# Block 1's down and gate products made inside the scan, one in each unit

## The chip, the cores and the metric

The kernel runs on one core of one Trainium2 chip. A core has TensorE (matrix products into the banks of PSUM), VectorE, ScalarE (activations), GpSimd (called POOL in the profile, it does not read PSUM) and SyncE, which issues transfers. They run side by side, each in its own order, and wait for one another on semaphores. The metric is the device time of one execution in microseconds. Before the change it is 612.0 us, the median of three runs (608.17 to 615.97).

## The reference, cut to what matters

Two blocks follow one another on `x` of 2 x 512 tokens with 256 channels. Block 0 (attention on sorted keys and a mixture of 64 experts) is not touched. Block 1 takes the normalized `xn` through a recurrence with 32 heads of 8 channels and through a feed-forward part with 640 hidden units, and adds both to `x`:

```python
xk, xv, xr, xg = (x + xx * m for m in (maa_k, maa_v, maa_r, maa_g))   # xx: the token before, less x
r, k, v = xr @ Wr.T, xk @ Wk.T, xv @ Wv.T
g = silu(xg @ Wg.T)
att = rc @ kc * w_mat                          # w_mat: decay below the diagonal, u on it, 0 above
yc = att @ vc + rc @ state * wb
new_state = ws * state + kc * wk @ vc
out = (groupnorm(y) * gamma + beta) * g @ Wo.T
ff = square(relu(xn @ w_fc.T)) @ w_proj.T      # with ternary weights
x = x + out + ff
```

## The kernel before

Tokens lie in eight tiles of 128 (`NT`), four for each of the two sequences. Everything is float32. Each engine's program is written out by hand, and its order is the order of the code; nothing is scheduled.

Ahead of block 1's scan TensorE works through this list. The feed-forward's first product fills hidden units by chunk and sequence (`s_ffp`); ScalarE takes the ReLU of each of the ten pieces into `hf` (`s_relu`) and between them makes the decay tables `wmask` by 32 exponentials. VectorE squares each piece (`square`, `s_sq`). `project_T` then makes keys and receptances with channels on the partitions (`s_kTp`, `s_rTp`), from mixtures that VectorE has made (`mixture(k)`, of x and of the difference `dif`; 0 for keys, 1 for receptances, 2 for values, 3 for gates). VectorE copies the keys out (line 1185) and multiplies the receptances by the decay (1192); ScalarE copies these into `rhead`, four times each with the other heads masked out (803). Then TensorE makes the feed-forward's down product, five matmuls to a tile (line 1311 is the helper `product`, so it stands on many rows), and VectorE adds each from PSUM to `xs` (`x2_add`, 1197). Transposes of the keys (1547), scaled by VectorE (1210), give `kn`; `project(2, ...)` gives the values (copied by ScalarE, 808), `project(3, ...)` the gates, of which ScalarE takes the tanh (813) and VectorE makes the silu (1220). POOL cuts `wmask` above the diagonal in one `affine_select` (591), VectorE puts `u` on its diagonal (1215). Only when all gates are ready does `scores(0)` start.

The scan has 16 units, two to a tile: unit u takes the heads `f = u % 2` of tile `u // 2`. TensorE makes four score products (1575), each on 32 rows of the array with 512 columns into banks 0 to 3; they run at the same time if they may start together. VectorE multiplies each by its mask into a ring (1289, `s_a1`). TensorE then makes the unit's outputs from state and masked scores (1585 and 1591) into bank 4 or 5, and the state product (1603); VectorE updates the state (1226, 1227). TensorE is one unit ahead with scores: unit u + 1's scores stand before unit u's outputs, and each waits for the mask that frees its bank. ScalarE copies the outputs (829); TensorE transposes them once in two units (1611), ScalarE copies these to `xn` (833). The group norm of earlier tiles lies between VectorE's masks: means (1242, 1245), then POOL subtracts (607), ScalarE squares (821), variances (1252, 1255), ScalarE's square root (817), and the scale (1262 to 1272). POOL multiplies by scale, gamma, beta and gate (617 to 623). Unit 8 begins the second sequence: VectorE clears the state (1280) after unit 7's outputs.

Behind the scan the eight gated tiles are transposed, multiplied by `Wo`, added to `xs` (1305) and stored.

Of the kernel before, what the change touches and what calls it, by code (L numbers as in the profile page):

```python
# [21 lines left out]
ALU = mybir.AluOpType  # L22
# [3 lines left out]
P = 128  # L26
# [54 lines left out]
def block_kernel(nc, x, consts, w_qk, w_v, w_gate, w_sh13, w_sh2, w_o0, w_13, w_2, maa, td_row, td_col, u_row,  # L81
# [12 lines left out]
    with ctx:  # L94
# [144 lines left out]
        w_head = carve(2 * DC * D, at=sc_at + 15 * N).rearrange("p (k c n) -> p k c n", k=2, c=DC)  # L239
        rw = v3(carve(2 * N), 2, N)  # L240
# [96 lines left out]
        s_wm1 = sem("decay_tables_exp")  # L337
# [10 lines left out]
        s_ffd = sem("ff_down_in_psum")  # L348
        s_x2 = sem("x2_ready")
# [158 lines left out]
        def _(pool):  # L508
# [77 lines left out]
            for k in range(2):  # L586
# [3 lines left out]
            pool.wait_ge(s_wm1, 1)  # L590
            nc.gpsimd.affine_select(out=wmask, in_=wmask, compare_op=ALU.is_ge, fill=0.0, base=-1,
                                    pattern=[[0, H1], [1, P]], channel_multiplier=-1).then_inc(s_wmc, 1)
# [16 lines left out]
            def gated(t):  # L609
# [14 lines left out]

            for t in range(NT):
# [3 lines left out]
                nc.gpsimd.tensor_copy(dst, vn[:, t, :].rearrange("p (g a c) -> p g a c", g=8, a=4)).then_inc(s_vd, 1)  # L629
                if t >= 2:  # L630
                    centred(t - 2)
                if t >= 3:
                    gated(t - 3)
            centred(NT - 2)
# [6 lines left out]
        def _(act):  # L641
# [137 lines left out]
            for b in range(B):  # L779
# [9 lines left out]
                for f in range(FC):  # L789
# [3 lines left out]
                    for h in range(4 * i, min(4 * i + 4, H1)):  # L793
                        last = nc.scalar.activation(wmask[:, h, :], const("pdist"), ACT.Exp, scale=edrow[:, h:h + 1])  # L794
                        if h == H1 - 1:
                            last.then_inc(s_wm1, 1)
# [46 lines left out]
        def _(dve):  # L843
# [307 lines left out]
            def square(i):  # L1151
                dve.wait_ge(s_relu, i + 1)
                h = hf[:, i % FC, (i // FC) * S:(i // FC + 1) * S]
                nc.vector.tensor_tensor(h, h, h, ALU.mult).then_inc(s_sq, 1)

            for i in range(FC):
                square(i)

# [8 lines left out]
            def mixture(k):  # L1167
                for c in range(DC):
                    ins = nc.vector.scalar_tensor_tensor(mix[:, k % 2, c * N:(c + 1) * N], dif[:, c, :],
# [9 lines left out]
            for i in range(FC, 2 * FC):  # L1179
                square(i)  # L1180

# [518 lines left out]
```

## Time and profile before

| what | us or share |
|---|---|
| median of three runs | 612.0 |
| the profiled execution's time | 605.34 |
| its span, first to last instruction | 603.6 |
| TensorE busy over the span | 75% |
| VectorE | 56% |
| ScalarE | 32% |
| POOL | 57% |
| mean granted TensorE clock | 0.895 of 2.4 GHz |

The profile is one execution. Busy time is the time in which an instruction of an engine was under way; matmuls are pipelined, so a busy TensorE is not one at its peak. A float32 product shows two records to a matmul. The chain of waits is followed back from the last instruction to what released each step. A row of the timeline gives start, length, engine, line and operation, the count, and in brackets the idle time before and what ended it. PEld is TensorE loading weights.

### The profile page before, as it was taken

The numbers are of one execution on the slowest core, as the hardware profiler recorded it, in microseconds if no ns is written. First come the engines' busy times: TensorE is split into PE (matmuls) and PEld (weight loads), VectorE is DVE, ScalarE is ACT, GpSimd is POOL, SyncE is SP. The second block draws the span as 40 slices with busy tenths as digits, with TensorE's granted clock in tenths as the row PEclk, the third lists the DMA queues.
The fourth block names the chain that finished last, engine by engine and source line by source line (L and its number), as shares of the span: only waits on it lengthen the run. The fifth ranks groups of instructions, "written<-read, shape, count | busy, mean of one in ns | idle before, by whom it ended". The sixth has DMA issues, their size and how long they took to land.

```text
span 603.6 us, 8476 instructions
## 1 busy us (share of the span) xinstructions
PE 453.7 (75%) x2288; PEld 281.1 (47%) x2288; DVE 340.7 (56%) x931; ACT 193.6 (32%) x512; POOL 343.3 (57%) x327
## 2 busy tenths in 40 slices
PE   2940860767778878887687778779687998899977
PEld 1620420344445445544455445447533587454545
DVE  4899985134444434444444444433467529598984
ACT  1423220233434334333343334422065413121112
POOL 6057777777777787777777777652123101023544
PEclk9975895599998888888989888989879999799997
DMA  8501618167887878788777777862600000000002
GB/s 307 211 24 32 168 24 222 43 165 170 193 201 187 204 199 190 179 198 208 192 191 204 196 189 190 212 145 62 202 9 2 0 0 1 1 1 2 2 2 70
DMA packets 49152, 75.40 MB, mean 125 GB/s; under 512 B 13721, under 2 KB 30457, under 8 KB 48953
## 3 DMA queue, kind: packets, MB, share of 16 engines
q1 hardware_dynamic: 32136, 53.74, 29.0%
q0 software_dynamic: 16992, 21.38, 19.7%
q8 instruction: 11, 0.18, 0.1%
q14 instruction: 13, 0.10, 0.1%
HBM read 58.31 MB, written 15.99 MB: 123 GB/s over the span
## 4 chain that ended last, share of the span: by engine, by line
POOL 33%; PE 25%; issue 17%; DMA 13%; DVE 8%; ACT 4%; SPq 0%; ACTq 0%; POOLq 0%; DVEq 0%
POOL big L543 15%; PE ps L1311 15%; POOL routed L557 9%; POOL big L550 7%; DMA routed<-big 6%; DMA big<-tok_tab,big 5%; PE ps L1575 4%; DVE big L1289 2%; PE ps L1316 2%; PE ps L1591 2%; DMA big<-in_maa 1%; ACT big L794 1%; DVE big L914 1%; DVE big L911 1%; DVE big L918 1%
## 5 line engine op out<-in xcount | busy, mean ns | idle before, releaser
L1311 PE MATMUL ps<-big 128*128 128x352 f32 (+4 forms) x768 | 223.2, 441 | 2.5 <-ACT big L708 0.9
L1311 PEld LDWEIGHTS ps<-big 128*128 128x128 f32 (+2 forms) x768 | 149.2, 202 | 58.1 <-issue 24.1
L543 POOL DMA_INDIRECT big<-val_tab,big x128 | 123.8, 967 | 62.5 <-issue 38.1
L557 POOL DMA_INDIRECT routed<-big x64 | 103.8, 1621 | 42.5 <-ACT big L718 25.9
L1316 PE MATMUL ps<-cst,big 128*128 128x128 f32 x144 | 31.3, 307 | 80.6 <-DMA big<-tok_tab,big 79.0
L1027 DVE COPY big<-ps 88x256 f32<-88x256 f32 x64 | 26.9, 421 | 91.3 <-PE ps L1403 90.2
L550 POOL DMA_INDIRECT big<-tok_tab,big x64 | 63.1, 986 | 19.5 <-issue 18.6
L1019 DVE SCALAR_TENSOR_TENSOR big<-big,ps 128x176 f32<-128x176 f32 x64 | 21.6, 338 | 84.5 <-ACT big L713 84.5
L708 ACT ACTIVATE big<-ps 128x256 f32<-128x256 f32 x64 | 24.5, 384 | 132.8 <-PE ps L1316 131.9
L1316 PEld LDWEIGHTS ps<-cst,big 128*128 128x128 f32 x144 | 16.7, 148 | 101.1 <-DMA big<-tok_tab,big 78.9
L1311 PE MATMUL ps<-xnT,big 128*128 128x512 f32 (+1 forms) x104 | 50.3, 641 | 2.1 <-ACT xnT L645 2.1
L713 ACT ACTIVATE big<-ps 128x176 f32<-128x176 f32 x64 | 20.3, 317 | 76.5 <-PE ps L1311 76.5
L1289 DVE TENSOR_TENSOR big<-ps,big 128x512 f32<-128x512 f32 x64 | 41.9, 677 | 2.5 <-PE ps L1575 2.1
L1575 PE MATMUL ps<-big 32*128 32x512 f32 x128 | 35.7, 673 | 3.0 <-DVE big L1289 2.0
L724 ACT ACTIVATE big<-ps 128x512 f32<-128x512 f32 x64 | 34.6, 599 | 0.5 <-PE ps L1420 0.4
L1311 PEld LDWEIGHTS ps<-xnT,big 128*128 128x128 f32 (+1 forms) x104 | 20.5, 203 | 27.7 <-issue 26.1
L718 ACT ACTIVATE big<-ps,big 128x256 f32<-128x256 f32 x64 | 30.0, 469 | 8.8 <-PE ps L1311 8.4
L1403 PE MATMUL ps<-cst,big 128*88 128x128 f32 x128 | 28.3, 307 | 0.0
L1316 PE MATMUL ps<-cst,xn 128*128 128x128 f32 x48 | 10.8, 352 | 20.4 <-DVE xn L879 17.7
L1403 PEld LDWEIGHTS ps<-cst,big 128*88 128x88 f32 x128 | 15.6, 134 | 21.1 <-issue 17.2
L596 POOL MEMSET big<- 128x2560 f32 x1 | 2.2, 2236 | 39.2 <-ACT big L808 39.2
L607 POOL TENSOR_TENSOR xn<-xn,gst 128x256 f32<-128x256 f32 x8 | 5.0, 629 | 33.5 <-DVE gst L1245 33.5
(179 smaller groups left out, 616.3 us busy)
## 6 DMA issues: line engine op xcount, KB each, us to landing
big<-in_w SPq DMA_DIRECT2D x64, 352.0 KB
big<-in_w SPq DMA_DIRECT2D x64, 176.0 KB
big<-q_dram SPq DMA_DIRECT2D x144, 32.0 KB
routed<-big POOLq DMA_DIRECT2D x2, 1152.0 KB
big<-val_tab,big POOLq DMA_INDIRECT x128, 2.3
big<-routed SPq DMA_DIRECT2D x4, 512.0 KB, 4.3
q_dram<-big SPq DMA_DIRECT2D x24, 64.0 KB, 1.8
tok_tab<-xn SPq DMA_DIRECT2D x1, 1280.0 KB, 5.2
```

What stands on the lines that cost most here:

```text
L543: nc.gpsimd.indirect_dma_start(vals[:, group, side, c, :], None, val_tab, bass.IndirectOffsetOnAxis(ap=vidxT[:, col:col + 1], axis=0))\
L550: nc.gpsimd.indirect_dma_start(xe[:, e % SLOTS, :], None, tok_tab, bass.IndirectOffsetOnAxis(ap=sidx[:, e:e + 1], axis=0))\
L557: nc.gpsimd.indirect_dma_start(routed[e % 2], bass.IndirectOffsetOnAxis(ap=sidx[:, e:e + 1], axis=0), ye[:, e % 2, :], None, compute_op=AL ...
L708: nc.scalar.activation(xeT[:, u % 2, :, :], PS[0][:, 0:D].rearrange("p (c n) -> p c n", c=DC), ACT.Copy).then_inc(s_xeT, 1)
L718: nc.scalar.activation(ye[:, u % 2, :], PS[3][:, 0:D], ACT.Copy, scale=gate).then_inc(s_y, 1)
L724: nc.scalar.activation(ex[:, c, :], PS[4 + c % 2][:, :], ACT.Exp).then_inc(s_ex, 1)
L1027: nc.vector.tensor_copy(heT[:, u % 2, :, :], PS[2][0:IC, 0:2 * P].rearrange("p (c n) -> p c n", c=2))\
L1289: nc.vector.tensor_tensor(aring[:, a % 8, :].rearrange("p (h n) -> p h n", h=4), PS[q][:, :].rearrange("p (h n) -> p h n", h=4), wmask[:, ...
L1311: last = nc.tensor.matmul(o, w, m, start=(n == 0), stop=(n == len(pairs) - 1))
L1316: last = nc.tensor.transpose(bank[:, c * P:(c + 1) * P], src[:, c * P:(c + 1) * P], ident)
L1403: last = nc.tensor.transpose(PS[2][0:IC, c * P:(c + 1) * P], hm[:, u % 2, c * IC:(c + 1) * IC], ident)
L1575: nc.tensor.matmul(PS[q][:, :], kT[rows, f, tok(t)], rhead[rows, f, :, tok(t)], start=True, stop=True).then_inc(s_a1p, 1)
```

## The change

Two products leave the stretch ahead of the scan. The down product of a tile is made in that tile's first unit and its gate product in the second, between two halves of the next unit's scores: quarters 0 and 1, the product, then quarters 2 and 3. The down product goes to bank 5, the gate product to bank 4, the two output banks, so that outputs now wait for the copy or the gate step that frees them. ScalarE copies the down sums from PSUM to `ffo`, two tiles long, because POOL now adds them to `xs` and can't read PSUM. ScalarE's tanh stands between the copies of the scan, VectorE's gate step behind the first mask of the next even unit. Squares go from VectorE to POOL, and the cut of `wmask` is made in two halves, the diagonals on VectorE likewise. The gates' mixture is written over `xnT`.

```diff
@@ POOL @@
+            def square(i):
+                pool.wait_ge(s_relu, i + 1)
+                h = hf[:, i % FC, (i // FC) * S:(i // FC + 1) * S]
+                nc.gpsimd.tensor_tensor(h, h, h, ALU.mult).then_inc(s_sq, 1)
+            def causal(i):
+                w = wmask[:, i * HH:(i + 1) * HH, :]
+                pool.wait_ge(s_wm1[i], 1)
+                nc.gpsimd.affine_select(out=w, in_=w, compare_op=ALU.is_ge, fill=0.0, base=-1,
+                                        pattern=[[0, HH], [1, P]], channel_multiplier=-1).then_inc(s_wmc, 1)
+            for i in range(4):
+                square(i)
+            causal(0)
+            square(4)
+            causal(1)
+            for i in range(FC, 2 * FC):
+                square(i)
...
-                    pool.wait_ge(s_g, NT)
+                pool.wait_ge(s_g, t + 1)
...
+            def x2_add(t):
+                pool.wait_ge(s_ffo, t + 1)
+                nc.gpsimd.tensor_tensor(xs[:, t, :], ffo[:, t % 2, :], xs[:, t, :], ALU.add).then_inc(s_x2, 1)
...
+                if t >= 1:
+                    x2_add(t - 1)
@@ ACT @@
+            def ff_copy(t):
+                act.wait_ge(s_ffd, t + 1)
+                if t >= 2:
+                    act.wait_ge(s_x2, t - 1)
+                nc.scalar.activation(ffo[:, t % 2, :], PS[5][:, 0:D], ACT.Copy).then_inc(s_ffo, 1)
+            def gate_tanh(t):
                 act.wait_ge(s_gp, t + 1)
-                if t == 0:
-                    act.wait_ge(s_knp, NT)
-                nc.scalar.activation(gn[:, t, :], PS[t % 4][:, 0:D], ACT.Tanh, scale=0.5).then_inc(s_gt, 1)
+                nc.scalar.activation(gn[:, t, :], PS[4][:, 0:D], ACT.Tanh, scale=0.5).then_inc(s_gt, 1)
...
                     u = 2 * t + f
+                    (ff_copy, gate_tanh)[f](t)
                     act.wait_ge(s_yTp, u + 1)
@@ DVE @@
-            for i in range(FC, 2 * FC):
-                square(i)
+            def diagonal(i):
+                dve.wait_ge(s_wmc, i + 1)
+                for h in range(i * HH, (i + 1) * HH):
+                    note(nc.vector.scalar_tensor_tensor(wmask[:, h, :], ident, urow[:, h:h + 1], wmask[:, h, :],
+                                                        ALU.mult, ALU.add))
+            diagonal(0)
...
-            for t in range(NT):
-                x2_add(t)
             mixture(3)
...
+                    if q == 0 and u >= 2 and not f:
+                        gate(u // 2 - 1)
@@ PE @@
-            pe.wait_ge(s_sq, 2 * FC)
-            for t in range(NT):
-                pe.wait_ge(s_kf, min(t + 1, 4))
-                if t >= 4:
-                    pe.wait_ge(s_x2, t - 3)
-                product(PS[t % 4][:, 0:D], [(hf[:, c, tok(t)], w_pj1[:, c, :]) for c in range(FC)]).then_inc(s_ffd, 1)
...
-            project(3, 3, 0, g_bank, s_gp)
+            def ff_down(t):
+                pe.wait_ge(s_sq, FC * (1 + t // TPB))
+                product(PS[5][:, 0:D], [(hf[:, c, tok(t)], w_pj1[:, c, :]) for c in range(FC)]).then_inc(s_ffd, 1)
+            def gate_product(t):
+                pe.wait_ge(s_mix, 4)
+                product(PS[4][:, 0:D], [(mixed(3, c, tok(t)), w5[:, 3, c, :]) for c in range(DC)]).then_inc(s_gp, 1)
+            def token_product(u):
+                pe.wait_ge(s_yT, u)
+                (ff_down, gate_product)[u % 2](u // 2)
...
-                if u >= 2:
-                    pe.wait_ge(s_yT, u - 1)
+                if u >= 1:
+                    pe.wait_ge(s_ffo if u % 2 else s_g, (u + 1) // 2)
...
-            pe.wait_ge(s_g, NT)
             pe.wait_ge(s_v1, NT)
-            scores(0)
+            scores(0, range(4))
             for u in range(UNITS):
                 if u + 1 < UNITS:
-                    scores(u + 1)
+                    scores(u + 1, (0, 1))
                 if u >= 2 and u % 2 == 0:
                     y_natural(u // 2 - 1)
+                token_product(u)
+                if u + 1 < UNITS:
+                    scores(u + 1, (2, 3))
                 outputs(u)
                 state_product(u)
```

In TensorE's program of before, units 2 and 3 of the scan read as follows (1575 scores, 1611 transposes of y, 1585 and 1591 outputs, 1603 the state product):

```order
L1575 MATMUL ps<-big 128x512 [waits scores_masked] x4
L1611 MATMUL ps<-cst,big 128x128 [waits yT_copied]
L1611 MATMUL ps<-cst,big 128x128
L1585 MATMUL ps<-big 128x128 [waits state_ready,yT_copied]
L1591 MATMUL ps<-big 32x128 [waits v1_placed,scores_masked]
L1591 MATMUL ps<-big 32x128 x15
L1603 MATMUL ps<-big 128x128 [waits state_ready]
L1575 MATMUL ps<-big 128x512 [waits scores_masked] x4
L1585 MATMUL ps<-big 128x128 [waits state_ready,yT_copied]
```

The four scores of a unit stand together. In the program of the change, the same place (1596 scores, 1632 transposes, 1338 the helper `product`, 1606 and 1612 outputs, 1624 the state product):

```order
L1596 MATMUL ps<-big 128x512 [waits scores_masked] x2
L1632 MATMUL ps<-cst,big 128x128 [waits yT_copied]
L1632 MATMUL ps<-cst,big 128x128
L1338 MATMUL ps<-big 128x256 [waits ff_square_done,yT_copied]
L1338 MATMUL ps<-big 128x256 x4
L1596 MATMUL ps<-big 128x512 [waits scores_masked] x2
L1606 MATMUL ps<-big 128x128 [waits state_ready,g1_ready]
L1612 MATMUL ps<-big 32x128 [waits v1_placed,scores_masked]
L1612 MATMUL ps<-big 32x128 x15
L1624 MATMUL ps<-big 128x128 [waits state_ready]
L1596 MATMUL ps<-big 128x512 [waits scores_masked] x2
L1338 MATMUL ps<-big,xnT 128x256 [waits mix_ready,yT_copied]
```

The scores stand in two pairs, with the five matmuls of a down product between them in an even unit and, where the piece ends, a gate product in an odd one; the outputs of an even unit wait for the gate step.

ScalarE's program of before, one tile of the scan (829 copy of y, 821 square, 817 square root, 833 copy of the transposed y):

```order
L829 ACTIVATE big<-ps 128x128 [waits y_nat_in_psum,yT_in_psum]
L821 ACTIVATE big<-xn 128x256 [waits group_means_subtracted]
L829 ACTIVATE big<-ps 128x128 [waits yT_in_psum]
L817 ACTIVATE gst<-gst 128x32 [waits group_var_ready]
L833 ACTIVATE xn<-ps 128x256 [waits y_nat_in_psum]
```

And of the change (840 copy of the down sums, 862 copy of y, 853 square, 844 tanh, 849 square root, 866 copy of the transposed y):

```order
L840 ACTIVATE big<-ps 128x256 [waits x2_ready,ff_down_in_psum]
L862 ACTIVATE big<-ps 128x128 [waits y_nat_in_psum,yT_in_psum]
L853 ACTIVATE big<-xn 128x256 [waits group_means_subtracted]
L844 ACT_TABLE_LOAD
L844 ACTIVATE big<-ps 128x256 [waits g1_in_psum]
L862 ACTIVATE big<-ps 128x128 [waits yT_in_psum]
L849 ACT_TABLE_LOAD
L849 ACTIVATE gst<-gst 128x32 [waits group_var_ready]
L866 ACTIVATE xn<-ps 128x256 [waits y_nat_in_psum]
```

The copy of the down sums and the tanh have come in, and with the tanh two loads of a function table to a tile, one ahead of the tanh and one ahead of the square root, where the program of before has one load in the whole scan. Over the scan the program of the change has 13 of them.

## Rows read from the trace of the kernel before

**Rows 1.** Chain of waits, 465 to 517 us: start, length, what

```profile
465.47 31.25 PE ps L1311 x112
...
501.45 13.98 PE ps L1311 x64
```

**Rows 2.** Windows: us, busy PE, PEld, DVE, ACT, POOL, clock, DMA

```profile
496.80:501.40 4.60, 2.14 (x17) 1.42 (x14) 4.60 (x9) 0.00 (x0) 0.00 (x0) 1.00 0.00 0
...
519.70:526.50 6.80, 6.80 (x49) 3.56 (x47) 3.58 (x7) 0.28 (x1) 0.00 (x0) 0.50 0.01 2
526.50:585.10 58.60, 56.09 (x658) 31.26 (x650) 53.30 (x135) 12.06 (x35) 20.98 (x34) 1.00 0.01 2
```

**Rows 3.** Timeline of VectorE ahead of the scan: start, length, instruction, idle before

```profile
463.04 3.09 DVE L1154 TENSOR_TENSOR big<-big 128x512 f32<-128x512 f32 x5
...
473.22 2.47 DVE L1169 SCALAR_TENSOR_TENSOR big<-big,xnT 128x1024 f32<-128x1024 f32 x2
...
479.48 0.69 DVE L1192 TENSOR_TENSOR big<-ps,wb 128x512 f32<-128x512 f32 x1 [1.02 <-PE ps L1311]
...
496.75 0.42 DVE L1197 TENSOR_TENSOR xs<-ps,xs 128x256 f32<-128x256 f32 x1 [1.73 <-PE ps L1311]
```

**Rows 4.** Timeline of ScalarE, ahead of and in the scan

```profile
476.33 9.36 ACT L803 ACTIVATE big<-ps,cst 128x512 f32<-128x512 f32 x16 [11.11 <-DVE big L1192]
...
535.88 1.28 ACT L817 ACT_TABLE_LOAD   x1
537.17 0.23 ACT L817 ACTIVATE gst<-gst 128x32 f32<-128x32 f32 x1
...
576.09 0.42 ACT L821 ACTIVATE big<-xn 128x256 f32<-128x256 f32 x1 [1.75 <-POOL xn L607]
...
589.50 0.42 ACT L821 ACTIVATE big<-xn 128x256 f32<-128x256 f32 x1 [2.80 <-POOL xn L607]
```

**Rows 5.** Timeline of TensorE's products in the scan

```profile
516.35 1.14 PE L1575 MATMUL ps<-big 32*128 32x512 f32 x8 [0.93 <-DVE big L1220]
...
576.37 0.49 PE L1585 MATMUL ps<-big 128*128 128x128 f32 x2
...
577.79 0.49 PE L1603 MATMUL ps<-big 128*128 128x128 f32 x2
578.21 2.50 PE L1575 MATMUL ps<-big 32*128 32x512 f32 x8
580.65 0.44 PE L1611 MATMUL ps<-cst,big 128*128 128x128 f32 x2
580.92 0.39 PE L1585 MATMUL ps<-big 128*128 128x128 f32 x2
...
583.99 1.08 PE L1591 MATMUL ps<-big 128*32 128x128 f32 x32 [1.25 <-DVE big L1289]
```

**Rows 6.** Timeline of TensorE's weight loads in the scan

```profile
579.59 0.29 PEld L1575 LDWEIGHTS ps<-big 32*128 32x128 f32 x2 [0.30 <-DVE big L1289]
580.64 0.20 PEld L1611 LDWEIGHTS ps<-cst,big 128*128 128x128 f32 x2 [0.76 <-issue]
```

**Rows 7.** Timeline of VectorE at the scan's start and in it

```profile
515.87 0.42 DVE L1220 SCALAR_TENSOR_TENSOR big<-big,ps 128x256 f32<-128x256 f32 x1 [0.44 <-ACT big L813]
...
551.93 0.27 DVE L1280 MEMSET big<- 128x256 f32 x1 [2.58 <-PE ps L1591]
...
573.44 0.68 DVE L1289 TENSOR_TENSOR big<-ps,big 128x512 f32<-128x512 f32 x1
...
575.18 0.17 DVE L1245 TENSOR_SCALAR gst<-gst 128x32 f32<-128x32 f32 x1
...
576.73 0.41 DVE L1252 TENSOR_REDUCE gst<-big 128x32 f32<-128x256 f32 x1
```

**Rows 8.** Timeline of POOL

```profile
463.02 6.81 POOL L591 TENSOR_SCALAR_AFFINE_SELECT big<-big 128x4096 f32<-128x4096 f32 x1 [16.13 <-ACT big L794]
...
575.43 0.63 POOL L607 TENSOR_TENSOR xn<-xn,gst 128x256 f32<-128x256 f32 x1 [4.31 <-DVE gst L1245]
```

More of the change, by code:

```diff
@@ L336, in block_kernel @@
         s_kdec = sem("key_decay_exp")
-        s_wm1 = sem("decay_tables_exp")
+        s_wm1 = [sem(f"decay_tables_exp{i}") for i in range(2)]
         s_wmc = sem("decay_mask_causal")
@@ L1148, in _ @@
             ln_apply(1, 1)
[L1151 to L1156, printed above, removed]
-                square(i)
             dve.wait_ge(s_xnT, 2 * NT)
@@ L1212, in _, with gate @@
                                         kdec.unsqueeze(2).broadcast_to([P, H1, HN]), ALU.mult).then_inc(s_kn, 1)
-            dve.wait_ge(s_wmc, 1)
-            for h in range(H1):
-                note(nc.vector.scalar_tensor_tensor(wmask[:, h, :], ident, urow[:, h:h + 1], wmask[:, h, :],
-                                                    ALU.mult, ALU.add))
+            diagonal(1)
             settle()
-            for t in range(NT):
+            def gate(t):
                 dve.wait_ge(s_gt, t + 1)
-                nc.vector.scalar_tensor_tensor(gn[:, t, :], gn[:, t, :], 1.0, PS[t % 4][:, 0:D], ALU.add, ALU.mult)\
+                nc.vector.scalar_tensor_tensor(gn[:, t, :], gn[:, t, :], 1.0, PS[4][:, 0:D], ALU.add, ALU.mult)\
                   .then_inc(s_g, 1)
@@ L1298, in _ @@
                     state_update(u - 1)
+            gate(NT - 1)
             for norm, t in ((group_variances, NT - 2), (group_scale, NT - 2), (group_means, NT - 1),
@@ L1520, in project_T @@
                             [(w_head[:, w, c, f * P:(f + 1) * P], mixed(k, c, half(n))) for c in range(DC)]).then_inc(done, 1)
-            def project(k, w, bank, bank_free, done):
-                for t in range(NT):
-                    bank_free(t)
-                    product(PS[bank + t % 4][:, 0:D], [(mixed(k, c, tok(t)), w5[:, w, c, :]) for c in range(DC)])\
-                        .then_inc(done, 1)
             pe.wait_ge(s_w5, 16)
@@ L1548, in _ @@
                 last.then_inc(s_knp, 1)
-            def v_bank(t):
+            pe.wait_ge(s_mix, 3)
+            for t in range(NT):
                 pe.wait_ge(s_kn, min(t + 5, NT))
@@ L1553, in v_bank, with scores @@
                     pe.wait_ge(s_v1, t - 3)
-            pe.wait_ge(s_mix, 3)
-            project(2, 2, 4, v_bank, s_v1p)
-            def g_bank(t):
-                if t < 4:
-                    pe.wait_ge(s_x2, t + 5)
-                else:
-                    pe.wait_ge(s_g, t - 3)
-            pe.wait_ge(s_mix, 4)
-            project(3, 3, 0, g_bank, s_gp)
-            def scores(u):
+                product(PS[4 + t % 4][:, 0:D], [(mixed(2, c, tok(t)), w5[:, 2, c, :]) for c in range(DC)])\
+                    .then_inc(s_v1p, 1)
+            def ff_down(t):
[7 more added lines that the diff above has]
+                (ff_down, gate_product)[u % 2](u // 2)
+            def scores(u, quarters):
                 t, f = divmod(u, 2)
-                for q in range(4):
+                for q in quarters:
                     a = 4 * u + q
```

22 lines of the change are left out of this document (11 added, 11 removed).

## The prediction

> **What bounds the kernel now.** The change lies in block 1, the last 160 us, so the chain of waits is read there first. It shows TensorE without a gap for 31.25 us from 465.47 and for 13.98 us from 501.45 [rows 1]: first key and receptance products (32 records), then the down products (80), later values and gates (64). The reader is to see that nothing else is ahead of the scan's first score at 516.35: every product taken out of this stretch shortens it. The windows by stage come next [rows 2]. In the scan VectorE is busy 53.30 of 58.60 us; TensorE's 56.09 is not work alone, since score products stand there that came one by one as masks freed their banks. The clock is 1.00 there, 0.50 from 519.7 to 526.5.
>
> Third, VectorE's timeline ahead of the scan [rows 3]: the receptance product is out when its last decay product starts, 479.48, and the last down sum is read at 496.75: 17.27 us for eight tiles, 2.16 each. Fourth, ScalarE [rows 4]: its sixteen copies that set heads apart end at 476.33 + 9.36 = 485.69, six microseconds behind the product, hidden by the down products today.
>
> Then what a scan unit asks of TensorE [rows 5, 6]. Four scores that may start together take 1.14. From the last score's weight load to the next instruction's (579.59 to 580.64) it is 1.05: that is what any group of scores costs, one or four. Outputs take 1.42 (576.37 to 577.79), the state product 0.42 (to 578.21), y's transposes 0.27 (580.65 to 580.92). The scores from 578.21 to 580.65 took 2.44 because they waited for masks; 1.4 of it is room. The scan is 516.35 to 583.99 + 1.08: 68.7 us, 8.6 for two units.
>
> **The change, part by part.**
>
> *Squares, masks and sums leave VectorE.* The five squares of 3.09 us began at 463.04 [rows 3] and were over before the first key product was out; TensorE began at 465.47 because of the ReLUs. Gain: nothing. In their place stand sixteen diagonals, and the eight x2 additions and the other sixteen diagonals lay behind TensorE. Nothing again, but one price: POOL's squares now run until about 475. POOL's one select took 6.81 us while VectorE's squares ran beside it [rows 3, 8]: the two engines can hold each other up. A square of 512 on POOL is estimated at 1.3 us, twice the 256-wide 0.63 of [rows 8]. The third mixture (473.22, on the path to the receptance copies) may wait for one: between 0 and 1.3; I take 0.6, about half a square, since the start falls anywhere in one.
>
> *Down and gate products leave the stretch ahead of the scan.* The values' start was 501.45. Now it waits for the head copies, 485.69 + 0.6 = 486.3, then for the fourth tile's transposes, its scaling, and the other four tiles' transposes at 0.27: 487.7. Mixture 3 (2.47 by the same form in [rows 3]) is done by 483, under the head copies; without that cover it would cost its 2.5. Values: 13.98/16 = 0.87 a tile, 7.0 in all, to 494.7; last copy, first score at 495.2. That is **-21.1**.
>
> *The clock.* From 479.5 to 486 TensorE has only a few transposes. Today's nearest pause, 496.8 to 501.4 with 2.14 us busy, left it at 1.00 [rows 2]; the sparse start of the scan went into 6.8 us of 0.50. So the values lose between 0 and 3.4 us (half of 6.8); I take **+1.7**, because the new pause is longer than today's and nearly empty.
>
> *The scan.* Scores are cut into two halves with a product between them, so that a unit pays 1.05 twice. Two units cost TensorE 4 x 1.05 + 2 x 1.42 + 2 x 0.42 + 0.27 + 2.16 + 0.87 = 11.2 us. VectorE has 8.6 plus a gate step of 0.42 [rows 7], so it goes under TensorE's time, and TensorE becomes the bound. Unit 0: first scores 1.14, second mask (0.68 each) done at 2.5, scores 3.6, down product 5.8, scores 6.8, outputs and state 8.7. Then seven pairs, 78.3; three missing state products, -1.3; at unit 8 the state's reset waits for unit 7's outputs, and the second mask comes 0.27 + 0.2 + 0.68 + 0.42 + 0.41 + 0.68 = 2.6 later (reset and its two short waits, mask, gate, reduction, mask; [rows 7]), TensorE standing; unit 15 2.7 (transposed copy, gate product, outputs). Sum 91.0 against 68.7: **+22.3**.
>
> Today's 68.7 already holds one stretch of half clock, under a scan that waited for VectorE. Where TensorE is the bound the same 6.8 us lose 3.4, or 0 if the first down product keeps the clock up: I take **+2.0**, a little over the middle, since the first units stay sparse.
>
> *New waits.* The gate's tanh stands on ScalarE between sqrt, so tables are loaded 13 times where [rows 4] has one load of 1.28. Behind each tanh queues the copy of y that outputs wait for, and VectorE's second mask of the next unit stands behind the gate step. The way round, from an odd unit's third mask: 573.44 to ScalarE's square at 576.09 (through VectorE 575.18 and POOL 0.63), 0.42, load 1.28, tanh 0.4 (as the square), gate 0.42, reduction 0.41, mask 0.68 [rows 4, 7, 8], together 6.3. TensorE asks for that mask 6.5 after the third one's start: 1.84 of outputs and state, less about 0.15 until the mask began, and the odd unit's 2 x 1.05 + 0.87 + 1.42 + 0.42 = 4.8. So the loads are just hidden, by 0.2; what exceeds that is paid in each pair. POOL's new additions (0.7 each) fit its idle time, 20.98 of 58.60 busy [rows 2].
>
> That sum takes a table switch at what the trace has: 535.88 + 1.28 = 537.16, the next activation at 537.17 [rows 4]. The Trainium skill ("ScalarE: Activation LUTs", section "What ACT_TABLE_LOAD costs") gives about 1283 ns and a drain of about 1380 besides, 2.66 us for every switch; its load agrees, no drain is seen behind the one in this trace. By the page, as an estimate, the sum would come to about 627.
>
> *Tail.* It begins with unit 15's outputs at 585.07; ScalarE's last square was at 589.50 [rows 4], 4.4 later. Now the gate's load and tanh hold back y's copy by about 0.7, and part of a sqrt load stands before the next copy; ScalarE's square comes at 5.8. **+1.4**, between 0 and 2.6 (two loads).
>
> **Sum:** -21.1 + 1.7 + 22.3 + 2.0 + 1.4 = +6.3. The profiled execution took 605.34 us (span 603.6), so 611.6; it lies 6.7 under the median 612.0 of the runs, on which scale it is **618**.
>
> **Rivals.**
> *TensorE takes the products in its gaps* (faster): the 1.4 us of room in each unit's scores [rows 5] holds them, VectorE stays the bound. Scan 68.7 + 8 x 0.42 + 2.2 for the first product: +5.6; -21.1 + 1.7 + 5.6 + 1.4 = -12.4, 599.6. For it: TensorE's figure is mostly waiting. Against: the cut costs 1.05 a unit, product and cut together 2.6 a unit against 1.4 of room.
> *Something between*: a half of scores overlaps its neighbour, and TensorE's pair falls to the way from gate to gate: VectorE's 8.6 + 0.42, less about 1 that it does behind the means, and 0.63 + 0.42 + 1.28 + 0.4 on POOL and ScalarE, 10.8 with the waits. 7 x 0.4 less: 615.
> *The table loads are on the path* (slower): ScalarE's way round lengthens, as when a load costs its 1.28 twice, or starts only when the gate product is there. Beyond the slack of 0.2 it is 1.1 for five pairs and 2.6 in the tail, +8: 626. It decides once the second mask comes more than 6.5 us after the third one's start. For it: 0.2 is thin, and there are 13 loads. Against: in the order the load itself waits for no product, and ScalarE is busy 12.06 of 58.60 us [rows 2]. The Trainium skill's page named above speaks for it.
> *The moves off VectorE do nothing*: that is in the sum.
>
> **How the numbers follow.** Likeliest, TensorE-bound scan: 0.58, own range 614 (no half clock) to 621 (all of both). Faster rival 0.12, between 0.10, loads on the path 0.20. A measurement of this kernel tells about 2% from no change: 599.8 and 624.2. Faster over 2%: 0.12; within 0.67; slower 0.21. The range, 600 to 627, takes in the middle cases and the lower half of the slow one, and leaves out 0.2.
>
> **What would show it.** Right: the first score near 495 to 498; a pair of units at 11.2 us with TensorE going from one instruction to the next and VectorE waiting for scores; a product record of 2.16 between two halves of scores; half clock while the values are made; unit 15 ending some 91 to 94 us after the first score. Wrong: scores' second half waiting for masks (VectorE still the bound), a pair under 10, or TensorE's first half idle behind the gate step (ScalarE's loads); a first score after 500 (mixture or head copies held up by POOL). The prediction falls with the 1.05 of a half: if two halves cost no more than the four did, most of the 22 is gone.

## The result: 12 us slower, and the profile after

The changed kernel takes 622.5 us (median of four runs, 620.58 to 624.85) where the kernel before takes 610.45 in the runs beside it (608.17 to 615.97). The ratio is 1.021, 95% interval 1.016 to 1.027. The profiled execution took 621.51 us with a span of 619.8, against 605.34 and 603.6. The profiled executions differ by 16.2 us, the medians by 12.05; the stages below are those of the profiled ones.

Block 1 begins for TensorE with the first transposes of `xn`. That row, before and then after (timeline of TensorE: start, length, instruction, idle before):

```profile
439.64 2.34 PE L1316 MATMUL ps<-cst,xn 128*128 128x128 f32 x8 [7.74 <-DVE xn L879]
```
```profile
442.61 2.34 PE L1343 MATMUL ps<-cst,xn 128*128 128x128 f32 x8 [7.48 <-DVE xn L912]
```

The 2.97 between them are block 0's, which the change does not touch, so stages are counted from this row:

| stage, us | before | after | predicted | measured |
|---|---|---|---|---|
| first transposes to first score | 76.71 | 59.20 | -19.4 | -17.5 |
| first score to the end of unit 15's outputs | 68.7 | 98.5 | +24.3 | +29.8 |
| from there to the end | 18.5 | 19.5 | +1.4 | +1.0 |
| sum | | | +6.3 | +13.3 |

Ahead of the scan, where [rows 3] and [rows 4] showed before, VectorE, ScalarE, TensorE and POOL now read:

```profile
466.05 9.98 DVE L1209 SCALAR_TENSOR_TENSOR big<-cst,big 128x128 f32<-128x128 f32 x16
475.95 2.48 DVE L1216 COPY big<-ps 128x512 f32<-128x512 f32 x4
...
493.69 4.29 DVE L1209 SCALAR_TENSOR_TENSOR big<-cst,big 128x128 f32<-128x128 f32 x16
```
```profile
467.62 0.60 ACT L818 ACTIVATE big<-ps 128x512 f32<-128x512 f32 x1 [1.12 <-PE ps L1338]
481.45 9.35 ACT L829 ACTIVATE big<-ps,cst 128x512 f32<-128x512 f32 x16 [13.23 <-DVE big L1223]
```
```profile
493.10 8.24 PE L1338 MATMUL ps<-big 128*128 128x256 f32 x32
501.81 1.14 PE L1596 MATMUL ps<-big 32*128 32x512 f32 x8 [0.47 <-ACT big L834]
```
```profile
466.02 2.00 POOL L602 TENSOR_SCALAR_AFFINE_SELECT big<-big 128x2048 f32<-128x2048 f32 x1 [7.47 <-ACT big L820]
467.99 5.26 POOL L597 TENSOR_TENSOR big<-big 128x512 f32<-128x512 f32 x5
```

The first sixteen diagonals take 9.98 us while POOL works beside them, the second sixteen 4.29 alone; the key copies queue behind the first. Behind the last ReLU (467.62) the head copies come 13.83 later, where they came 11.71 later before. The values, from 493.10, begin at half clock.

In the scan, one pair of units on TensorE (units 2 and 3) and the restart at unit 8:

```profile
517.41 1.13 PE L1596 MATMUL ps<-big 32*128 32x512 f32 x4
518.47 0.44 PE L1632 MATMUL ps<-cst,big 128*128 128x128 f32 x2
518.74 2.32 PE L1338 MATMUL ps<-big 128*128 128x256 f32 x10
520.99 1.13 PE L1596 MATMUL ps<-big 32*128 32x512 f32 x4
522.05 0.49 PE L1606 MATMUL ps<-big 128*128 128x128 f32 x2
522.47 1.08 PE L1612 MATMUL ps<-big 128*32 128x128 f32 x32
523.48 0.49 PE L1624 MATMUL ps<-big 128*128 128x128 f32 x2
523.90 1.13 PE L1596 MATMUL ps<-big 32*128 32x512 f32 x4
524.96 1.13 PE L1338 MATMUL ps<-big,xnT 128*128 128x256 f32 x4
526.02 1.13 PE L1596 MATMUL ps<-big 32*128 32x512 f32 x4
...
528.92 1.13 PE L1596 MATMUL ps<-big 32*128 32x512 f32 x4
...
550.11 1.08 PE L1612 MATMUL ps<-big 128*32 128x128 f32 x32
552.39 3.33 PE L1596 MATMUL ps<-big 32*128 32x512 f32 x4 [1.21 <-DVE big L1312]
555.65 0.69 PE L1632 MATMUL ps<-cst,big 128*128 128x128 f32 x2
556.13 4.39 PE L1338 MATMUL ps<-big 128*128 128x256 f32 x10
```

From 517.41 to 528.92 is 11.51 us with no wait on TensorE: four halves of scores at 1.06 (start to the next start), a down product 2.25, a gate product 1.06, outputs, state and transposes. Before, two units took 8.6 on the mean (68.7 us for sixteen, [rows 5]). At unit 8 the wait for the masks is followed by products that take twice their time. The windows show the clock of those places (columns as in [rows 2]):

```profile
485.20:495.40 10.20, 5.78 (x20) 4.63 (x21) 5.66 (x16) 5.94 (x11) 0.00 (x0) 0.50 0.00 0
505.70:509.10 3.40, 3.40 (x9) 2.67 (x9) 1.02 (x2) 0.00 (x0) 0.00 (x0) 0.50 0.00 0
553.50:560.30 6.80, 6.67 (x15) 4.02 (x14) 3.21 (x9) 0.61 (x2) 0.00 (x0) 0.50 0.01 2
515.00:596.00 81.00, 79.66 (x680) 45.50 (x676) 52.55 (x135) 29.24 (x56) 24.94 (x39) 0.96 0.00 1
```

TensorE is busy 79.66 of 81.00 us, VectorE 52.55: the bound went from VectorE to TensorE. The pages' costliest groups say the same: before its masks VectorE stood idle 2.5 us in the kernel before, and 26.6 us after, 26.0 of it for scores.

```profile
L1289 DVE TENSOR_TENSOR big<-ps,big 128x512 f32<-128x512 f32 x64 | 41.9, 677 | 2.5 <-PE ps L1575 2.1
```
```profile
L1312 DVE TENSOR_TENSOR big<-ps,big 128x512 f32<-128x512 f32 x64 | 42.2, 681 | 26.6 <-PE ps L1596 26.0
```

### The profile page after: what moved, and what is told of

The parts are those of the page before. It is cut to its first block, busy times and chain, and to the rows that moved or that the text cites. A ratio compares the mean times of both kernels' runs of the same rounds, so it can differ in the third digit from the quotient of the medians.

```text
span 619.8 us, 8530 instructions
## 1 busy us (share of the span) xinstructions
PE 466.1 (75%) x2288; PEld 282.0 (46%) x2288; DVE 336.7 (54%) x913; ACT 211.9 (34%) x532; POOL 357.1 (58%) x346
## 4 chain that ended last, share of the span: by engine, by line
POOL 31%; PE 26%; issue 15%; DMA 14%; DVE 8%; ACT 4%; SPq 0%; ACTq 0%; POOLq 0%; DVEq 0%
POOL big L546 16%; PE ps L1338 12%; POOL routed L560 8%; DMA routed<-big 7%; POOL big L553 7%; DMA big<-tok_tab,big 6%; PE ps L1596 6%; PE ps L1612 2%; PE ps L1343 2%; DVE big L1209 2%; ACT big L829 2%; DMA big<-in_maa 1%; DVE big L1195 1%; PE ps L1606 1%; ACT big L820 1%
## 5 line engine op out<-in xcount | busy, mean ns | idle before, releaser
L1338 PE MATMUL ps<-big 128*128 128x352 f32 (+3 forms) x736 | 222.0, 450 | 2.7 <-ACT big L734 0.9
L1338 PEld LDWEIGHTS ps<-big 128*128 128x128 f32 (+1 forms) x736 | 145.5, 208 | 58.5 <-issue 24.3
L1343 PE MATMUL ps<-cst,big 128*128 128x128 f32 x144 | 32.1, 313 | 80.6 <-DMA big<-tok_tab,big 79.2
L553 POOL DMA_INDIRECT big<-tok_tab,big x64 | 63.3, 990 | 19.5 <-issue 18.3
L1312 DVE TENSOR_TENSOR big<-ps,big 128x512 f32<-128x512 f32 x64 | 42.2, 681 | 26.6 <-PE ps L1596 26.0
L1596 PE MATMUL ps<-big 32*128 32x512 f32 x128 | 37.6, 647 | 2.6 <-DVE big L1312 2.0
L1338 PE MATMUL ps<-big,xnT 128*128 128x256 f32 (+1 forms) x128 | 30.2, 382 | 4.3 <-ACT xnT L872 3.9
L1338 PEld LDWEIGHTS ps<-xnT,big 128*128 128x128 f32 (+1 forms) x104 | 20.4, 202 | 27.7 <-issue 26.1
L646 POOL TENSOR_TENSOR xs<-big,xs 128x256 f32<-128x256 f32 x8 | 5.8, 725 | 39.8 <-ACT big L840 39.8
L1338 PEld LDWEIGHTS ps<-big,xnT 128*128 128x128 f32 x128 | 22.3, 204 | 12.7 <-issue 5.0
L1430 PEld LDWEIGHTS ps<-cst,big 128*88 128x88 f32 x128 | 15.9, 136 | 24.0 <-issue 20.1
```

The costliest lines, as they stand in the source:

```text
L553: nc.gpsimd.indirect_dma_start(xe[:, e % SLOTS, :], None, tok_tab, bass.IndirectOffsetOnAxis(ap=sidx[:, e:e + 1], axis=0))\
L1312: nc.vector.tensor_tensor(aring[:, a % 8, :].rearrange("p (h n) -> p h n", h=4), PS[q][:, :].rearrange("p (h n) -> p h n", h=4), wmask[:, ...
L1338: last = nc.tensor.matmul(o, w, m, start=(n == 0), stop=(n == len(pairs) - 1))
L1343: last = nc.tensor.transpose(bank[:, c * P:(c + 1) * P], src[:, c * P:(c + 1) * P], ident)
L1430: last = nc.tensor.transpose(PS[2][0:IC, c * P:(c + 1) * P], hm[:, u % 2, c * IC:(c + 1) * IC], ident)
L1596: nc.tensor.matmul(PS[q][:, :], kT[rows, f, tok(t)], rhead[rows, f, :, tok(t)], start=True, stop=True).then_inc(s_a1p, 1)
```

## The experiments

All are measured like the change; times are medians, ratios are to the kernel before in the same set of runs (medians 610.9 to 611.6). The stages of all profiled executions, read as above ("ReLU to score" is from the last ReLU to the first score, "outputs 0" from the first score to unit 0's first output from masked scores, a pair from that point in unit 2 to the same in unit 4, then 10 to 12). The time is the median; the stages are those of one profiled execution, which took 599.35 us for "uncut" and 595.42 for "both", the fastest of each, so the columns do not add up to the medians:

| kernel | ReLU to score | outputs 0 | pairs | units 6 to 8 | scan | tail | time |
|---|---|---|---|---|---|---|---|
| before | 51.7 | 6.5 | 7.2, 8.3 | 10.0 | 68.7 | 18.5 | 611 |
| after | 34.2 | 9.1 | 11.5, 11.5 | 16.4 | 98.5 | 19.5 | 622.5 |
| uncut | 34.2 | 5.2 | 9.5, 10.4 | 11.0 | 80.7 | 20.4 | 604.0 |
| diagonals moved | 32.6 | 9.1 | 11.5, 11.5 | 16.5 | 98.5 | 19.7 | 620.2 |
| no tables | 34.2 | 9.1 | 11.5, 11.5 | 16.4 | 98.5 | 17.1 | 618.9 |
| moves only | 51.7 | 5.2 | 7.2, 8.3 | 11.4 | 67.2 | 17.6 | 610.7 |
| uncut in units 0, 8 | 32.6 | 5.2 | 11.5, 11.5 | 10.9 | 89.4 | 19.1 | 611.2 |
| uncut, diagonals moved | 32.6 | 5.2 | 9.5, 10.4 | 11.0 | 80.7 | 20.7 | 603.2 |
| uncut, scaling later | 32.6 | 5.2 | 9.5, 10.5 | 10.9 | 80.6 | 21.5 | 605.5 |
| uncut, 4 downs ahead | 33.0 | 7.3 | 8.6, 10.4 | 11.3 | 81.6 | 20.0 | 603.5 |
| uncut, 3 downs ahead | 37.7 | 5.2 | 8.4, 10.4 | 11.4 | 77.8 | 20.1 | 603.3 |
| uncut, SiLU | 34.3 | 5.2 | 9.5, 10.4 | 10.7 | 80.7 | 20.5 | 603.9 |
| both | 32.8 | 5.2 | 8.4, 10.4 | 10.0 | 74.9 | 20.1 | 601.3 |

### Scores uncut, the product first

```diff
-                if u + 1 < UNITS:
-                    scores(u + 1, (0, 1))
                 if u >= 2 and u % 2 == 0:
                     y_natural(u // 2 - 1)
                 token_product(u)
                 if u + 1 < UNITS:
-                    scores(u + 1, (2, 3))
+                    scores(u + 1, range(4))
```

> The kernel after, but in each unit the token product (down or gate) stands first and then all four score passes of the next unit run in one piece, not cut into two halves. Theory 1: TensorE's own time bounds the scan, and the cut costs because a pass of a half waits to drain (1.06 us for each half of two passes, four passes uncut as in the kernel before). Then a pair of units takes 9.4 to 10.3 us in place of 11.52, the scan is 9 to 15 us shorter than in the changed kernel, and the time is 607 to 613 us (about that of before). Rival: the score passes are paced by what reads them (VectorE's masking frees their banks), or the cut is free. Then the pair stays at 11.3 to 11.7 us and the time at 620 to 624 us.

603.98 us (599.35 to 608.65), ratio 0.989, interval 0.985 to 0.994: 18.5 us under the changed kernel, more than the theory wanted, and below the kernel before. TensorE's timeline in unit 0, then the product and scores of an even unit, then those of an odd unit:

```profile
496.51 1.14 PE L1596 MATMUL ps<-big 32*128 32x512 f32 x8 [0.47 <-ACT big L834]
497.58 2.43 PE L1338 MATMUL ps<-big 128*128 128x256 f32 x10
499.94 1.46 PE L1596 MATMUL ps<-big 32*128 32x512 f32 x8
...
517.06 2.32 PE L1338 MATMUL ps<-big 128*128 128x256 f32 x10
519.31 1.14 PE L1596 MATMUL ps<-big 32*128 32x512 f32 x8
...
522.28 1.13 PE L1338 MATMUL ps<-big,xnT 128*128 128x256 f32 x4
523.34 1.86 PE L1596 MATMUL ps<-big 32*128 32x512 f32 x8
```

Four scores occupy 1.07 (519.31 to the next instruction at 520.38), as long as two did. The first two pairs fall by 2.0, later ones by 1.1, because from there the odd unit's scores wait for masks (1.86). The 2.0 are what the rows of the halves say, twice 1.06. That gives some 9 of the 17.8 us off the scan. The edit both joins the scores and puts the product ahead of them; joined scores with the product behind them were not run. The rest lies in unit 0 and at unit 8, and the clock is 1.00 through the whole scan:

```profile
496.50:577.20 80.70, 78.31 (x822) 49.43 (x822) 59.95 (x152) 29.58 (x61) 29.75 (x45) 1.00 0.01 2
```

### Uncut in units 0 and 8 only

The same edit under `u % 8 == 0`; the other units keep the change's order.

> The kernel after, with the product-first, uncut order in units 0 and 8 only; in the other fourteen units the scores stay cut. It splits what the uncut order gained (17.8 us in the scan) into the price of the cut and that of TensorE's pauses. Theory 1 (pauses): in units 0 and 8 TensorE stands still for the masks in front of the first half, and its clock falls to half behind that; with the product in that pause both stretches at half clock in the scan are gone, the first outputs come 3 to 4 us earlier and the step from unit 6's outputs to unit 8's falls from 16.4 to 11.5 us or less, the other pairs stay at 11.52 us: scan 89 to 91 us, time 612 to 615 us. Rival (the cut alone): two units less cut, 2.1 us off the scan, the stretches at half clock still there: 619 to 621 us.

611.22 us, ratio 1.006 (1.002 to 1.011). Scan 89.4, in the theory's range, the time just under its 612 to 615; pairs stay at 11.5. Unit 0 gives 3.9 us, the step from unit 6 to 8 gives 5.5, and both stretches of half clock are gone (windows over unit 0 and over unit 8):

```profile
499.00:511.00 12.00, 11.90 (x112) 7.03 (x114) 8.52 (x16) 1.37 (x5) 4.10 (x5) 1.00 0.00 1
547.00:559.00 12.00, 12.00 (x107) 6.87 (x105) 10.03 (x27) 5.42 (x11) 4.51 (x7) 1.00 0.00 0
```

So the 17.8 us split into 9.1 for units 0 and 8, where TensorE stood still and then ran slowly (about 2.1 of them are the cut of these two units), and 8.7 for the cut in the other fourteen.

### Squares, causal halves and diagonals alone

The kernel before with `square` and `causal` on POOL and `diagonal(0)` ahead of the key copies, as in the change; all products stay ahead of the scan.

> The kernel before, with one part of the change alone: squares on GpSimd in place of VectorE, the causal step of the masks cut into halves, and the first eight diagonals moved ahead. The down and gate products stay ahead of the scan as in the kernel before. Theory 1: the squares were hidden work on VectorE, and GpSimd's are later than the down products want them and hold up VectorE's diagonals beside them; the time is 611 to 614 us (0 to 3 us over that of before). Rival: VectorE freed of squares lets the copies and the products behind them come earlier: 605 to 608 us.

610.7 us, ratio 1.003 (0.998 to 1.007): nothing, as predicted for these moves (between this run's theory, 611 to 614, and its rival, 605 to 608). The head copies are just as late as in the changed kernel:

```profile
466.91 0.60 ACT L808 ACTIVATE big<-ps 128x512 f32<-128x512 f32 x1 [1.12 <-PE ps L1320]
480.73 9.36 ACT L819 ACTIVATE big<-ps,cst 128x512 f32<-128x512 f32 x16 [13.22 <-DVE big L1204]
```
```profile
465.33 9.98 DVE L1190 SCALAR_TENSOR_TENSOR big<-cst,big 128x128 f32<-128x128 f32 x16
```

The delay belongs to the moves (13.82 behind the last ReLU against 11.71), and the down products ahead of the scan hide it; without them it is on the path.

The scan of this run has the order of the kernel before, with no product in TensorE's waits. The windows over unit 0 and behind unit 8's wait, then unit 8 in the kernel before:

```profile
518.70:526.30 7.60, 6.77 (x60) 3.13 (x60) 5.67 (x11) 0.28 (x1) 0.00 (x0) 1.00 0.01 2
553.00:559.80 6.80, 6.80 (x45) 4.10 (x44) 5.26 (x15) 0.87 (x4) 0.77 (x2) 0.50 0.00 0
```
```profile
552.90:560.00 7.10, 7.01 (x56) 3.65 (x56) 6.99 (x20) 1.31 (x4) 1.66 (x4) 1.00 0.01 2
```

In the kernel before the clock fell in unit 0 ([rows 2]) and not at unit 8; here it is the other way round. An empty wait makes the fall likely, but not certain.

### Diagonals moved back

`diagonal(0)` placed next to `diagonal(1)`, behind the scaled keys.

> The kernel after, but VectorE makes the first eight diagonals of the decay masks directly ahead of the last eight, behind the scaled keys, so that they do not run beside GpSimd's squares, and the key and receptance copies do not wait for them. Theory: the eight held-up diagonals (part of 9.98 us for sixteen) delay the start of the scan by about 2.1 us; moved, they cost 2.1 us where nothing waits. Then key copies, head copies and the first score come 1.5 to 2.5 us earlier and the time is 618.5 to 620.5 us. Rival: the first score waits for TensorE's own chain of products, or what is gained there is lost because the diagonals stand later: 621 to 623 us.

620.2 us (615.18 to 623.38), ratio 1.014 (1.009 to 1.018): in the expected range, but not told apart from the changed kernel by these intervals. Behind the last ReLU the head copies are back at 11.71. But in this execution the clock fell once more, ahead of the edited place, and the ReLU came 2.1 later:

```profile
458.30:461.70 3.40, 3.28 (x4) 1.51 (x5) 3.27 (x5) 0.07 (x1) 0.00 (x0) 0.52 0.00 0
```
```profile
468.85 0.60 ACT L818 ACTIVATE big<-ps 128x512 f32<-128x512 f32 x1 [1.12 <-PE ps L1338]
480.56 9.35 ACT L829 ACTIVATE big<-ps,cst 128x512 f32<-128x512 f32 x16 [11.11 <-DVE big L1222]
```

The kernel uncut in units 0 and 8 has the early diagonals, had the same late ReLU, and shows 11.71 too. There the diagonals were not held up; POOL's select was, 4.72 us where it takes 2.00 in the changed kernel:

```profile
463.48 4.28 DVE L1209 SCALAR_TENSOR_TENSOR big<-cst,big 128x128 f32<-128x128 f32 x16
```
```profile
464.91 4.72 POOL L602 TENSOR_SCALAR_AFFINE_SELECT big<-big 128x2048 f32<-128x2048 f32 x1 [8.93 <-ACT big L820]
```

So it is in all nine executions with early diagonals. In six (the changed kernel, uncut, no tables, moves only, 3 downs ahead, SiLU) the diagonals start 0.02 or 0.03 us behind the select and take 9.98; in the three with the late ReLU (uncut in units 0 and 8, scaling later, both) they start 1.4 to 1.5 us ahead of it, take 4.28, and the select takes 4.67 to 4.72. The hold-up costs the head copies 2.1 us in the first case and nothing in the second. No kept trace has the moved diagonals with the early ReLU, so what moving them gains is not shown, and the time may lie in the expected range by chance. Uncut scores with moved diagonals:

> The kernel with uncut scores in all units and the token product first, and also with the first eight diagonals moved down to the last eight. In the run with the moved diagonals alone the head copies stood 2.1 us earlier behind the last copy of the up products (11.71 us, as in the kernel before, in place of 13.83) and the first score 1.55 us earlier; the start of block 1 had lost as much in that run ahead of the edited place. Theory: the two gains add up: 601.5 to 603 us, 1.5 to 2.1 us under the uncut kernel alone. Rival: the gain is lost at the values or in the scan: 603.5 to 605 us.

603.24 us (599.22 to 604.36), ratio 0.989 (0.981 to 0.998), against 603.98: no gain that these runs can show.

### No table changes

```diff
-                nc.scalar.activation(g[1], g[0], ACT.Sqrt).then_inc(s_gs, 1)
+                nc.scalar.activation(g[1], g[0], ACT.Square).then_inc(s_gs, 1)
```

> The kernel after, with the square root of the group norm replaced by a square (so its normalisation is wrong: the square root is left out). ScalarE then needs no change of table inside the scan. Theory: the changes of table (1.28 us each) stand in ScalarE's idle time and TensorE never waits for them; the time is 620 to 622.5 us and the pair stays at 11.4 to 11.6 us. Rival: ScalarE's table changes lie on the path through the gate's bank: the pair is about 1 us shorter and the time 612 to 615 us.

618.88 us (618.52 to 621.21), ratio 1.012 (1.006 to 1.019). The scan is 98.52 us against 98.51, every pair 11.51 or 11.52: in it the table changes cost nothing. The tail falls by 2.4; ScalarE's last square comes 3.5 us behind the scan's end instead of 4.9, which is the loads' part, and the tail's half clock is 3.4 us long instead of 6.8. The rival (612 to 615) falls; the time lies 1.1 us under the theory's range, as the tail is shorter.

### What bounds the pairs of the uncut kernel

VectorE's scaling steps put one unit later, so that they lie in even units:

```diff
-                        t, odd = divmod(u - 3 - stage, 2)
+                        t, odd = divmod(u - 3 - stage - stage // 2, 2)
```

> The kernel with uncut scores and the token product first, in which VectorE makes the scaling step of each tile's group norm one unit later, in an even unit, where TensorE has a down product, and not in an odd one, where it has a gate product. In the uncut kernel the first two pairs of units take 9.52 us and the later ones, where the norm runs beside, 10.4. Theory: in odd units VectorE's row of masks and norm steps (3.55 us) is longer than what TensorE has to do between two units' scores (2.96 us), and frees the score banks late; with the step moved the later pairs take 9.5 to 9.8 us, the tail grows by 0 to 1 us, and the time is 600 to 602.5 us. Rival: the later pairs are TensorE's own, or wait for something else (ScalarE's copy of y behind table changes): pairs stay at 10.4, time 603.5 to 605.5 us.

605.54 us, ratio 0.995 (0.991 to 0.999): the rival's time. Odd units fall from 4.75 to 4.02 us as the theory said (their scores now take 1.14 in place of 1.86), but even units rise from 5.66 to 6.45, since now their scores wait, 2.12 in place of 1.14:

```profile
543.15 2.32 PE L1338 MATMUL ps<-big 128*128 128x256 f32 x10
545.41 2.12 PE L1596 MATMUL ps<-big 32*128 32x512 f32 x8
```

VectorE's row is the bound in whichever unit the scaling lies. Its gate step taken away (SiLU on ScalarE, straight from the product; `gate` goes):

```diff
-                nc.scalar.activation(gn[:, t, :], PS[4][:, 0:D], ACT.Tanh, scale=0.5).then_inc(s_gt, 1)
+                nc.scalar.activation(gn[:, t, :], PS[4][:, 0:D], ACT.Silu).then_inc(s_g, 1)
```

> The uncut kernel with the gate made by one ScalarE step (its SiLU function, which is half of (tanh(x/2)+1)x) straight from the product, so that VectorE has no gate step (0.42 us in each even unit) and its bank is free one hop earlier. Theory: the later pairs (10.4 us) are bound by VectorE's row of masks, norm and gate steps over both units, as the run with the scaling step moved suggests (odd unit 4.75 to 4.02, even unit 5.66 to 6.45, pair unchanged); with 0.42 us less the pair falls to 9.9 to 10.1 us and the time to 600.5 to 602.5 us. Rival: they are bound by TensorE or by ScalarE's row with its table changes: pairs at 10.3 to 10.5, time 603 to 605 us.

603.92 us, ratio 0.988 (0.981 to 0.995), pairs 10.4: the theory fails here. The gate step is in the even unit, which has TensorE's down product to hide it; the odd unit still takes 4.75, in which the scaling and the means lie.

### Down products ahead of the scan again

In the uncut kernel with moved diagonals, tiles 0 to 3 get their down product behind the key transposes, and VectorE adds it at once:

```diff
+                if t < 4:
+                    pe.wait_ge(s_kf, t + 1)
+                    pe.wait_ge(s_sq, FC * (1 + t // TPB))
+                    product(PS[t][:, 0:D], [(hf[:, c, tok(t)], w_pj1[:, c, :]) for c in range(FC)]).then_inc(s_ffd, 1)
```

> The uncut kernel with the moved diagonals, in which the down products of the first four tiles are made ahead of the scan again, in the time in which TensorE waits for the head copies (its idle time there is about 7 us; the four products are 9.2 us at full clock), and VectorE adds them at once; in the first four tiles the even units have no product. Theory: the first four pairs fall from 9.5 to 11 us to the 8.0 to 8.5 us of the kernel before (6 to 8 us off the scan), the time ahead of the scan grows by 1 to 3 us, part of which comes back because the clock does not fall before the values: 596 to 600 us. Rival: the products ahead hold up the values by their whole time (and the adds hold up VectorE): 601 to 605 us, no gain over the run with uncut scores and moved diagonals.

603.53 us, ratio 0.990 (0.985 to 0.995): the rival's time, for another reason. The four products cost only 0.4 us ahead of the scan (33.0 against 32.6): they fill TensorE's pause, and the values run at full clock. But unit 0 then has no product, TensorE stands for the masks, and the half clock is back:

```profile
501.60:505.60 4.00, 2.27 (x11) 0.90 (x12) 3.85 (x12) 0.02 (x1) 2.98 (x3) 1.00 0.00 0
505.60:512.40 6.80, 6.80 (x45) 4.25 (x44) 3.74 (x8) 0.28 (x1) 0.00 (x0) 0.50 0.00 0
```

The masks also wait for the moved diagonals. With tiles 1 to 3 ahead and unit 0 keeping its product, and the diagonals as in the change:

> The uncut kernel in which the down products of tiles 1, 2 and 3 are made ahead of the scan, in TensorE's pause before the values, and those of tile 0 and of tiles 4 to 7 stay in the scan; the diagonals stand as in the changed kernel. In the run with four products ahead the time to the first score grew by 0.4 us only, but unit 0 had nothing in its pause and ran at half clock (first outputs 7.31 us behind the first score in place of 5.24), and the masks waited for the moved diagonals. Theory: with a product in unit 0 the pause is filled, first outputs come at 5.2 us, there is no half clock there, the pairs that begin with units 2, 4 and 6 lose 1 to 2 us each, and the time is 599 to 602 us against 604 of the uncut kernel. Rival: VectorE's row of masks and norm steps bounds those pairs whatever TensorE has to do, and the time stays at 603 to 605 us.

603.3 us (597.85 to 604.27), ratio 0.983 (0.975 to 0.992): the rival's time. But the scan is 2.9 us shorter than the uncut kernel's, just under the 3 to 6 of the theory's three pairs, and unit 0 has no half clock; a stretch of 3.4 us at 0.50 fell from 534.3 on, in unit 6, which has no product. Ahead of the scan 3.6 us went, because the half clock fell on the products there (first one 4.47 instead of 2.32):

```profile
484.63 4.47 PE L1346 MATMUL ps<-big 128*128 128x256 f32 x10
```

With SiLU besides:

> The last two edits together. If both theories hold the gains add up where they lie in different units: 597 to 600 us. If VectorE's row bounds all pairs, only the second edit counts: 600 to 603 us.

601.28 us (595.42 to 602.92), ratio 0.983 (0.976 to 0.990), the lowest median of all. In the profiled execution the same stretch ran at full clock and the diagonals were not held up, so the time from the last ReLU to the first score is 4.9 us shorter, 2.1 of it at the head copies; neither comes from the edited lines. The scan is 2.9 us shorter. The pair from unit 4 to 6 falls from 9.65 to 8.33: without SiLU VectorE stood 1.11 us there for the tanh behind its table load, so where an even unit has no product, the gate step does count. By their intervals this one and the uncut kernel can't be told apart for certain; both beat the kernel before.

## Why the prediction was right, and where it was low

It said 618, range 600 to 627, and most likely within 2%. 622.5 lies in the range and shows its likeliest case's mechanism, but it is above that case's own 614 to 621, and 2.1% slower (1.6 to 2.7), so that the 2% are not borne out. Against the 610.45 of the runs beside it the change costs 12.05 us, nearly twice the forecast's 6.3: the way and the bound were right, the size was low, and the width of the range took that in. Of its signs, TensorE without a wait in the pairs and VectorE waiting for scores came true; unit 15 ended 98.5 us behind the first score and not 91 to 94, and the first score, 498.8 when the 2.97 us of block 0 are taken off, was just past 495 to 498.

- **Squares, sums, masks off VectorE: nothing.** Right for squares and masks by the run with the moves alone; the sums' move was not run by itself. The 0.6 us for POOL beside VectorE was the wrong place: not the third mixture but the sixteen diagonals were held up, 9.98 us instead of 4.29, and the head copies came 2.15 later. The step knew that the two engines hold each other up and priced only one neighbour of the squares. The Trainium skill ("SBUF — State Buffer", section "SBUF: two separate sides") states that a VectorE operation with two SBUF inputs and a GpSimd one that reads SBUF lock each other out of a shared pair of ports for whole instructions. The rows agree, 5.7 us lost beside 7.3 us of POOL's work, and so does the reverse, the select's 4.72 in place of 2.00 beside diagonals that had started first.
- **-21.1 ahead of the scan and +1.7 of clock.** -17.5 together instead of -19.4: 1.5 us from that hold-up, which other executions of such kernels do not have, and 0.4 from the clock. The half clock was forecast for the values; it lay from 485.2 to 495.4, so that the last five transposes took 2.37 (1.51 in the run with four products ahead, at full clock) and the values 8.24 (7.14).
- **A pair at 11.2.** 11.52. A half at 1.06 was right, and it is what the forecast hung on; the gate product is 1.06 and not 0.87, the down product 2.25 and not 2.16. Those came from the values' and down products' rows ahead of the scan, where like products follow one another; alone between others each costs 0.1 to 0.2 more. Seven pairs: 2.2 us.
- **Unit 0 with +2.0 of half clock.** 10.57 against 10.7: right. All seven executions with a product in that pause kept 1.00, which bears out the reason, TensorE sparse at the start. But the run with the moves alone left the pause empty and kept 1.00 too, so the term could have been nothing, and that a middle value hit is in part luck.
- **Unit 8, +2.6.** The step that failed most: measured 5.75 (16.43, plus two missing state products of 0.42, less 11.52), 3.2 more. The wait itself was foreseen; that the clock falls behind it, 6.8 us at 0.50 (the down product 4.39 there and not 2.32), was not, though [rows 2] showed the same behind the scan's sparse start. The trace of before could not settle it: there the clock stayed at 1.00 at this place.
- **Tail +1.4.** +1.0. The run without table loads puts 1.35 of the tail on them.
- **Rival, loads on the path (626).** Refuted in the scan by the run without table loads. For the table change the Trainium skill ("ScalarE: Activation LUTs", section "What ACT_TABLE_LOAD costs") would add a drain to each load. The changed kernel's trace shows 1.28 us and the tanh 0.01 behind it, which speaks against the drain here:

```profile
536.76 1.28 ACT L844 ACT_TABLE_LOAD   x1
538.05 0.38 ACT L844 ACTIVATE big<-ps 128x256 f32<-128x256 f32 x1
```

- **Rival, products fit in TensorE's gaps (599.6).** False for the change, and nearly what the uncut order gives (604.0, scan +12.0): the products' 26.5 us (eight times 2.25 and 1.06) do go in part into room that TensorE had: the scan grows by 12.0 for them. The forecast's reason against this rival, the 1.06 of each half, was the right one.

## What to carry to other kernels

A product put among small passes is priced with what it breaks up: two scores cost as much as four, so cutting the group cost about 11 us here, while ahead of the uncut groups about half of the products' time was absorbed. When TensorE becomes the bound, look for each place where it still waits: work put into that pause can pay twice, once for its own time and once where the clock would have fallen behind the pause. A move off one engine is priced by what then runs beside it and which of the two starts first, and by whether the next edit takes the cover away.

## What the chip showed that was not expected

- VectorE's diagonals of two SBUF operands took 9.98 us for sixteen beside POOL's select and squares when the select had started 0.02 us or more ahead, and 4.28 when they had started 1.4 us ahead of it; then the select took 4.7 us in place of 2.00.
- Behind TensorE's waits for masks the clock stood at 0.50 for 3.4 us in unit 0 of the changed kernel (505.7 to 509.1) and for 6.8 at unit 8. With a product in the wait it stayed at 1.00 in unit 0 of all seven executions so built. With none it fell in five of six in unit 0 (not with the moves alone) and in four of five at unit 8 (not in the kernel before).
- Executions differ by where the clock falls: the last ReLU of block 1 starts 25.0 to 25.2 us behind its first transposes in seven and 26.8 to 27.1 in six. Each of the six has one more stretch of 3.4 us near half clock ahead of that ReLU (0.52 from 458.3 to 461.7 in the one shown), the seven have none there.
